# Two of a batch's four scatters move into the next attention step, scatters and gathers stand singly in GpSimd's program, and scale_wqkv goes behind low_part

## The chip, the cores and the metric

The kernel runs on one core of one Trainium2 chip. The metric is the device time in microseconds of one execution. Three executions of the kernel before took 956.85, 956.36 and 955.01 us; the median is 956.36.

The engines are named as the profile names them: PE is TensorE (PEld its weight loads), DVE is VectorE, ACT is ScalarE, POOL is GpSimd, and SP (SyncE) issues most DMAs. SPq and ACTq are the DMA queues of SP and ACT.

## The reference

```python
def reference(x, Wq, bq, Wk, bk, Wv, bv, Wo, bo, qn_w, kn_w, router_w, expert_weights, c, wmod):
    # x: [32, 256, 128]; 16 heads of 8; 32 experts of 128 x 128, two per token
    mod = (silu(c) @ wmod).reshape(32, 6, 1, 128)
    sa, ca, ga, sb, cb, gb = (mod[:, i] for i in range(6))
    ga, gb = at_least(ga, 0.25), at_least(gb, 0.25)        # by size, the sign kept
    h = layernorm(x) * (1 + ca) + sa
    qg = h @ Wq + bq                                       # q, and 16 gates
    Q, K = rmsnorm(q, qn_w), rmsnorm(h @ Wk + bk, kn_w)    # over a head's 8
    attn = softmax(Q @ K.T / sqrt(8))
    out = (attn @ V) * sigmoid(gate)
    x = x + ga * (out @ Wo + bo)
    h = layernorm(x) * (1 + cb) + sb
    rw = softmax(h @ router_w.T)                           # over 32 experts
    out = sum over a token's two best experts of (h * rw_e) @ expert_weights[e]
    return x + gb * out
```

All is float32. The sum over experts is written in the reference as a loop over all 32 with the weights of the others zero.

## The kernel before

Every engine has its own program, written by hand and unrolled in full, and the engines meet only at semaphores. The work goes by batches of 256 tokens (two tiles of 128). The program is a run of steps `s` = 0, 1, ..., each of which handles nine batches at once, each in another phase: `b0` is batch s, `b1` is batch s-1, and so on to `b8`. A step is `attention_step` up to s = 34, and `drain_step` from s = 35 (`DRAIN`) on. In a step, each engine runs a fixed list of small tasks in the order in which they are written there; a task begins with its waits and ends by raising a semaphore. So the order of lines in `attention_step` of POOL is the order of POOL's instructions, and a task that waits holds up all behind it.

The tasks that this text speaks of:

- `scale_wqkv(b0)` on POOL (L766, tile wq_b) scales the weights of the projections by the batch's modulation; PE's `project` (L1914) of the next step uses them.
- `norm_qk(b0, t)` on POOL (L784, qn) ends the step; PE's `transpose_qk` waits for it.
- `low_part(b1)` on POOL (L797, parts) makes the third part of q and k, which are split into three bf16 parts. SP stores the parts in `q_d` and `k_d` in HBM (L602) and loads them again as `q_aug` and `k_aug`, in the layout in which PE's `scores_q` (L1941, mx_ps) of the next batch reads them.
- `scores_q(b, h)` gives the maxima: DVE's `max_head` (L1401, negmax) reads mx_ps. When all 16 heads have theirs, POOL's `max_lead` (L804, mlead), `max_lead_wide` (L811) and `max_rest` (L817, both msplit) split them in two parts, PE's `transpose_max` (L1950) transposes these, ACT copies them (L1087, mrows), and SP stores them into `q_aug` as rows, so that `scores_k` (L1976, st_ps) subtracts the maximum itself. ACT's `exp_head` (L1093, pr) follows.
- `probs_v(b3, g)` on PE (L1990, o_ps) is 16 matmuls for a group of four heads, ACT's `out_transposed` (L1099, oT) copies the result, and the next `probs_v` waits for it, since there is one o_ps.
- `x_plus_bias` (L825, xga), `scale_wo` (L834, wo_b) and `copy_v` (L755, v_aug) are POOL's other small tasks of attention; `scale_ln2` (L841, h2a) and `shift_ln2` (L850, h) write the second norm's result into `h2`.
- The router: DVE finds each token's two best experts (`one_hot`, L1463), POOL makes `mask` (`chosen`, L867), PE counts, and DVE works out the row of each token and expert, `slot` (L1504). `keep_slot` (L899), `keep_index` (L884), `chosen_ranks` (L876, ohr) and `keep_weights` (L891, p_all) keep parts of it; `less_largest` (L858, L859) prepares the softmax.
- `scatter(b, k)` on POOL (L909, xs_d<-h,slot), k = 0 to 3, is one indirect DMA that writes 128 rows of h2 to the places of their experts in HBM: four of them per batch. The first waits for slot. Thirty of the 32 batches go this way, in chunks that end at batches 8, 16, 24 and 30 (`CUTS`); the last two are computed densely.
- When a chunk's rows are all there, SP loads them by units of expert rows (L650, xs_sb<-xs_d), PE transposes and multiplies them (L2121, L2140), and ACT stores the results (ys_d).
- `gather(n, ks)` on POOL (L924, yg<-ys_d,gidx) reads the results back by token, four indirect DMAs per batch, and DVE combines them. In attention steps this is done for one batch per step from s = 25 on; all other batches' gathers are in the drain and behind it. `table` is DVE's reckoning of a chunk's units (L1519 nunit is of it).

In a step with gathers, POOL's list before has gather 0 and scatter 3 of the batch before at its head, and gather 3 and the scatters 0, 1 and 2 near its end, in front of `norm_qk`.

Of the kernel before, what the change touches and what calls it, by code (L numbers as in the profile page):

```python
# [146 lines left out]
def combined_in(s):  # L147

    return COMBINED_IN.get(s, [])
# [71 lines left out]
def build(nc, x, Wq, bq, Wk, bk, Wv, bv, Wo, bo, qn_w, kn_w, router_w, expert_w, c_in, wmod, out):  # L221
# [16 lines left out]
    with ctx:  # L238
# [280 lines left out]
        def past_first(task, b):  # L519

            if b is not None and not (isinstance(b.n, int) and b.n == 0):
                task(b)
# [207 lines left out]
        def _(gp):  # L730
# [97 lines left out]
            @of_batch  # L828
            def scale_wo(b):

                wait(gp, xo_ld[b.par], 32 * (b.nth + 1))
                wait(gp, wo_ps, b.n - 1)
                gp.nop(nofuse=True)
                nc.gpsimd.tensor_tensor(wo_b[:, b.par], wo[:], mod_o[:, b.par, 0, :], ALU.mult).then_inc(wob_d, 1)  # L834
# [93 lines left out]
            def gather_in(s, *ks):  # L928

                for n in combined_in(s):  # L930
                    gather(n, ks)

            def attention_step(s, ahead, b0, b1, b2, b3, b4, b5, b6, b7, b8):

                gather_in(s, 0)
                scatter(b7, 3)
                x_plus_bias(b4)
                scale_wo(b4)
                copy_v(b2)
                keep_slot(b7)  # L940
                past_first(scale_wqkv, b0)
                low_part(b1)
                gather_in(s, 1)
                chosen(b6)
                scale_ln2(b5)
                keep_index(b6)
                gather_in(s, 2)
                chosen_ranks(b6)
                shift_ln2(b5)
                max_lead(b2)  # L950
                max_lead_wide(b2)
                max_rest(b2)
                gather_in(s, 3)
                scatter(b6, 0)
                scatter(b6, 1)
                keep_weights(b8)
                scatter(b6, 2)
                less_largest(b6)
                norm_qk(b0, 0)
                norm_qk(b0, 1)  # L960

            def drain_step(s, ahead, b0, b1, b2, b3, b4, b5, b6, b7, b8):

                if s == DRAIN:
                    scatter(b7, 3)
                gather_in(s, 0, 1)
                for k in range(TOPK * TB):
                    scatter(b6, k)
                gather_in(s, 2, 3)
# [1320 lines left out]
```

## Time and profile before

| | kernel before |
|---|---|
| median of 3 runs | 956.36 us |
| the profiled execution | 961.56 us, of it the span 959.8 us |
| busy share of the span | PE 78%, DVE 71%, ACT 59%, PEld 54%, POOL 53% |
| chain that ended last | PE 40%, DVE 17%, issue 13%, other or unknown queue 11%, DMA 8%, POOL 1% |
| POOL's gathers (L924) | 120, mean 990 ns |
| POOL's scatters (L909) | 120, mean 1004 ns |

The span runs from the first to the last instruction. A busy share is an average over stages: steps with scatters alone, steps with scatters and gathers, and the drain. "Idle before, releaser" is the time for which an engine stood still in front of an operation, and what ended it; "remote" is a releaser that the profile doesn't see as one of the engines, and "issue" is time in which the engine waited for nothing that the profile shows. "issue" in brackets behind a POOL DMA is the gap in front of it.

In the profile a step is read from POOL's `norm_qk` to the next one. Steps 16 to 24 lie from 331 to 529 us; steps 25 to 31, with gathers, from 529 to 702; the last three attention steps from 702 to about 773.

### The profile page before, as it was taken

To read this page: it belongs to the slowest core of one execution; us is meant where nothing else is said; L and a number is where in the kernel's file an instruction comes from. 1 tells how busy PE (TensorE), PEld (TensorE's weight loads), DVE (VectorE), ACT (ScalarE), POOL (GpSimd) and SP (SyncE) were. 2 spreads that over 40 slices of the span, in tenths; PEclk is the share of its full clock that TensorE was granted. 3 is DMA by queue.
4 is the path that set the end of the run, shared out by engine and by line. 5 is a ranking of instruction groups with operands and counts; after the bars stand their busy time and mean duration, and the time that the engine had idled before them with its cause. 6 is when DMAs were issued, how large, how long until landed. Compare 5 with 4: busy or idle time off the path is not lost.

```text
span 959.8 us, 23375 instructions
## 1 busy us (share of the span) xinstructions
PE 746.7 (78%) x6334; PEld 517.7 (54%) x6334; DVE 677.2 (71%) x2015; ACT 562.7 (59%) x1300; POOL 508.2 (53%) x846
## 2 busy tenths in 40 slices
PE   4668989888887899888888888898887753636666
PEld 1235655555554566665656556565665542535665
DVE  4767888778787888788877778799775353602566
ACT  3156877666675788777777777676664622513100
POOL 5112455566555555556455666666664545363353
PEclk8589999999898999999999999999888966857788
DMA  5445455466444667676566767666554343747422
GB/s 155 112 101 152 109 134 154 114 144 150 126 117 115 163 167 190 179 178 173 157 168 173 198 160 185 164 162 165 150 149 122 115 132 101 219 127 220 140 82 83
DMA packets 178001, 141.70 MB, mean 148 GB/s; under 512 B 19540, under 2 KB 162612, under 8 KB 177876
## 3 DMA queue, kind: packets, MB, share of 16 engines
q1 hardware_dynamic: 122804, 99.54, 40.5%
q10 hardware_dynamic: 47392, 24.92, 9.0%
q0 software_dynamic: 7680, 15.74, 6.1%
q8 instruction: 57, 0.93, 0.4%
q14 instruction: 68, 0.56, 0.2%
HBM read 81.77 MB, written 57.80 MB: 145 GB/s over the span
## 4 chain that ended last, share of the span: by engine, by line
PE 40%; DVE 17%; issue 13%; another core or an unknown queue 11%; DMA 8%; SPq 5%; ACT 4%; POOL 1%; DVEq 0%; ACTq 0%; POOLq 0%
PE mx_ps L1941 10%; PE st_ps L1976 8%; PE o_ps L1990 6%; DVE negmax L1401 6%; DMA k_aug<-k_d 4%; PE st_ps L2140 3%; PE misc L1999 3%; DMA k_d<-parts 3%; PE misc L1914 2%; ACT pr L1093 2%; SPq L602 1%; PE mx_ps L2140 1%; SPq L650 1%; PE st_ps L2121 1%
## 5 line engine op out<-in xcount | busy, mean ns | idle before, releaser
L1401 DVE TENSOR_REDUCE negmax<-mx_ps 128x2 f32<-128x512 f32 x512 | 338.5, 686 | 115.6 <-PE mx_ps L1941 58.0
L1093 ACT ACTIVATE pr<-st_ps 128x512 f32<-128x512 f32 x512 | 286.2, 600 | 77.0 <-PE st_ps L1976 72.7
L1941 PE MATMUL mx_ps<-k_aug,q_aug 126*128 126x256 bf16 x1024 | 199.8, 288 | 61.6 <-DVE negmax L1401 28.0
L1976 PE MATMUL st_ps<-q_aug,k_aug 128*128 128x256 bf16 x1024 | 191.1, 286 | 0.6 <-ACT pr L1093 0.3
L1990 PE MATMUL o_ps<-pr,v_aug 128*32 128x256 f32 x2048 | 143.4, 399 | 41.2 <-issue 33.7
L1941 PEld LDWEIGHTS mx_ps<-k_aug,q_aug 126*128 126x128 bf16 x1024 | 84.4, 100 | 151.2 <-issue 140.5
L924 POOL DMA_INDIRECT yg<-ys_d,gidx x120 | 118.8, 990 | 88.9 <-DVE yb L1631 38.8
L909 POOL DMA_INDIRECT xs_d<-h,slot x120 | 120.4, 1004 | 54.6 <-DVE slot L1504 28.7
L1976 PEld LDWEIGHTS st_ps<-q_aug,k_aug 128*128 128x128 bf16 x1024 | 102.3, 105 | 28.9 <-issue 9.7
L1990 PEld LDWEIGHTS o_ps<-pr,v_aug 128*32 128x32 f32 x2048 | 56.5, 111 | 91.9 <-issue 71.9
L1099 ACT ACTIVATE oT<-o_ps 128x256 f32<-128x256 f32 x128 | 49.2, 385 | 85.3 <-remote 49.5
L784 POOL TENSOR_TENSOR qn<-qkvg,rstd 128x256 f32<-128x256 f32 x64 | 39.1, 635 | 80.5 <-DVE rstd L1317 80.5
L797 POOL TENSOR_TENSOR parts<-rest,parts 128x512 bf16<-128x512 f32 x32 | 37.0, 1157 | 58.9 <-ACT parts L1081 58.9
L1914 PE MATMUL misc<-wq_b,hT 128*128 128x400 f32 x128 | 58.7, 547 | 3.2 <-DVE x L1432 2.2
L2121 PE MATMUL st_ps<-ident,xs_sb 128*128 128x128 f32 x248 | 43.0, 304 | 19.7 <-DMA xs_sb<-xs_d 18.1
L1150 ACT ACTIVATE xsT<-st_ps 128x512 f32<-128x512 f32 x62 | 36.6, 595 | 35.8 <-PE st_ps L2121 22.6
L1999 PE MATMUL misc<-ident,oT 128*128 128x128 f32 x256 | 43.8, 300 | 11.3 <-ACT oT L1099 8.4
L2140 PE MATMUL mx_ps<-we,xsT 128*128 x200 | 38.7, 358 | 13.8 <-issue 11.5
L2121 PEld LDWEIGHTS st_ps<-ident,xs_sb 128*128 128x128 f32 x248 | 33.0, 159 | 22.0 <-issue 21.3
L2140 PEld LDWEIGHTS mx_ps<-we,xsT 128*128 128x128 f32 x200 | 35.6, 268 | 16.6 <-issue 16.4
L1370 DVE TENSOR_TENSOR qkvg<-misc,bias_p 128x400 f32<-128x400 f32 x64 | 36.0, 564 | 12.0 <-PE misc L1914 6.5
L1586 DVE TENSOR_TENSOR q_aug<-misc,h2Td 128x512 f32<-128x512 f32 x32 | 21.3, 687 | 32.4 <-remote 23.4
(192 smaller groups left out, 1286.7 us busy)
## 6 DMA issues: line engine op xcount, KB each, us to landing
xs_sb<-xs_d SPq DMA_DIRECT2D x248, 64.0 KB
ys_d<-ys_sb ACTq DMA_DIRECT2D x62, 256.0 KB
q_aug<-q_d SPq DMA_DIRECT2D x64, 192.0 KB
mod_o<-mod_d SPq DMA_DIRECT2D x32, 256.0 KB
bias_p<-bias_d SPq DMA_DIRECT2D x32, 200.0 KB
q_d<-parts SPq DMA_DIRECT2D x32, 192.0 KB
k_d<-parts SPq DMA_DIRECT2D x32, 192.0 KB
k_aug<-k_d SPq DMA_DIRECT2D x64, 96.0 KB
```

What stands on the lines that cost most here:

```text
L909: nc.gpsimd.indirect_dma_start(xs_d[chunk.set], bass.IndirectOffsetOnAxis(ap=slot[:, b.par, k:k + 1], axis=0), h2[:, b.par, k % TB, :], No ...
L924: nc.gpsimd.indirect_dma_start(yg[:, n % FB, k, :], None, ys_d[chunk.c], bass.IndirectOffsetOnAxis(ap=gidx[:, pair:pair + 1], axis=0)).the ...
L1093: nc.scalar.activation(pr[:, h % PR], st_ps[score_bank(b, h)][:], ACT.Exp, scale=SCALE).then_inc(exp_d, 1)
L1099: nc.scalar.activation(oT[:, g, :], o_ps[:, 0:NT], ACT.Copy).then_inc(oT_d, 1)
L1401: v.tensor_reduce(negmax[:, :, h], mx_ps[h % 2][:], AX.X, ALU.max, negate=True).then_inc(mx_d, 1)
L1914: t_.matmul(bank[:, 0:QKVG], hT[:, t * P:(t + 1) * P], wq_b[:, b.par], start=True, stop=True).then_inc(qkv_ps, 1)
L1941: last = t_.matmul(mx_ps[h % 2][:, qc], q_aug[b.par][0:MROW, h, qc * P:(qc + 1) * P], k_aug[b.par][0:MROW, h, :], start=True, stop=True)
L1976: last = t_.matmul(st_ps[score_bank(b, h)][:, kc], k_aug[b.par][:, h, kc * P:(kc + 1) * P], q_aug[b.par][:, h, :], start=True, stop=True)
L1990: last = t_.matmul(o_ps[32 * j:32 * j + VW, 0:NT], v_aug[b.par][:, kc, h, :], pr[:, h % PR, kc, :], start=(kc == 0), stop=(kc == TB - 1))
L1999: last = t_.transpose(bank[:, g * P:(g + 1) * P], oT[:, g, qc * P:(qc + 1) * P], ident[:])
L2121: last = t_.transpose(in_bank(g)[:, k * P:(k + 1) * P], xs_sb[:, g % XB, k, :], ident[:])
L2140: last = t_.matmul(out_bank(g)[:, k * P:(k + 1) * P], xsT[g % XB][:, k * P:(k + 1) * P], we[:, bass.ds(columns[k], P)], start=True, stop=True)
```

## The change

Only POOL's lists are edited. In `attention_step`, scatter 2 of a batch moves from the end of a step to the head of the next one, where scatter 3 already was; scatter 3 moves behind `keep_slot`. Gather 0 goes behind `scale_wo`, and gather 3 in front of `max_lead`. `keep_weights` stands between scatters 0 and 1. `scale_wqkv` goes behind `low_part`. At the first drain step the batch that is in flight has two scatters left instead of one.

```diff
@@ def attention_step(s, ahead, b0, b1, b2, b3, b4, b5, b6, b7, b8):
-                gather_in(s, 0)
-                scatter(b7, 3)
+                scatter(b7, 2)
                 x_plus_bias(b4)
                 scale_wo(b4)
+                gather_in(s, 0)
                 copy_v(b2)
                 keep_slot(b7)
+                scatter(b7, 3)
+                low_part(b1)
                 past_first(scale_wqkv, b0)
-                low_part(b1)
                 gather_in(s, 1)
                 chosen(b6)
                 scale_ln2(b5)
@@
                 gather_in(s, 2)
                 chosen_ranks(b6)
                 shift_ln2(b5)
+                gather_in(s, 3)
                 max_lead(b2)
                 max_lead_wide(b2)
                 max_rest(b2)
-                gather_in(s, 3)
                 scatter(b6, 0)
+                keep_weights(b8)
                 scatter(b6, 1)
-                keep_weights(b8)
-                scatter(b6, 2)
                 less_largest(b6)
                 norm_qk(b0, 0)
                 norm_qk(b0, 1)
@@ def drain_step(s, ahead, b0, b1, b2, b3, b4, b5, b6, b7, b8):
                 if s == DRAIN:
+                    scatter(b7, 2)
                     scatter(b7, 3)
                 gather_in(s, 0, 1)
```

POOL's rows at the head of a step with gathers, before (L766 is scale_wqkv, L797 low_part, L924 a gather, L909 a scatter):

```order
L784 TENSOR_TENSOR qn<-qkvg,rstd 128x2x16x8 x2
L924 DMA yg<-ys_d,gidx 128x128
L909 DMA xs_d<-h,slot 69632x128
L825 TENSOR_TENSOR xga<-x_o,mod_o 128x256
L834 TENSOR_TENSOR wo_b<-wo,mod_o 128x128
L755 COPY v_aug<-qkvg 128x32x8
L899 CAST slot_all<-slot 128x4
L766 TENSOR_TENSOR wq_b<-wqkv,caT 128x400
L797 TENSOR_TENSOR parts<-rest,parts 128x2x256
L924 DMA yg<-ys_d,gidx 128x128
L867 TENSOR_TENSOR mask<-oh 128x64
```

The same place after:

```order
L784 TENSOR_TENSOR qn<-qkvg,rstd 128x2x16x8 x2
L909 DMA xs_d<-h,slot 69632x128
L825 TENSOR_TENSOR xga<-x_o,mod_o 128x256
L834 TENSOR_TENSOR wo_b<-wo,mod_o 128x128
L924 DMA yg<-ys_d,gidx 128x128
L755 COPY v_aug<-qkvg 128x32x8
L899 CAST slot_all<-slot 128x4
L909 DMA xs_d<-h,slot 69632x128
L797 TENSOR_TENSOR parts<-rest,parts 128x2x256
L766 TENSOR_TENSOR wq_b<-wqkv,caT 128x400
L924 DMA yg<-ys_d,gidx 128x128
L867 TENSOR_TENSOR mask<-oh 128x64
```

The pair of gather and scatter behind qn is taken apart, a second scatter stands ahead of low_part, and scale_wqkv has gone behind it.

POOL's rows at the end of the same step, before (L804 to L817 are max_lead, max_lead_wide and max_rest, L891 keep_weights, L858 less_largest):

```order
L850 TENSOR_TENSOR h<-h2a,mod_o 128x256
L804 CAST mlead<-negmax 128x32
L811 CAST msplit<-mlead 128x2x16
L817 TENSOR_TENSOR msplit<-negmax,mlead 128x2x16
L924 DMA yg<-ys_d,gidx 128x128
L909 DMA xs_d<-h,slot 69632x128 x2
L891 TENSOR_TENSOR p_all<-elg,rsum 128x4
L909 DMA xs_d<-h,slot 69632x128
L858 TENSOR_TENSOR dlg<-lg,top 128x2x32
```

and after:

```order
L850 TENSOR_TENSOR h<-h2a,mod_o 128x256
L924 DMA yg<-ys_d,gidx 128x128
L804 CAST mlead<-negmax 128x32
L811 CAST msplit<-mlead 128x2x16
L817 TENSOR_TENSOR msplit<-negmax,mlead 128x2x16
L909 DMA xs_d<-h,slot 69632x128
L891 TENSOR_TENSOR p_all<-elg,rsum 128x4
L909 DMA xs_d<-h,slot 69632x128
L858 TENSOR_TENSOR dlg<-lg,top 128x2x32
```

Behind msplit stand two DMAs with one operation between them, where there were four with one operation between; one of the four now stands ahead of mlead, and one is in the next step.

## Rows read from the trace of the kernel before

**Rows 1.** Busy time, share of the span and instructions of each engine.

```profile
PE 746.7 (78%) x6334; PEld 517.7 (54%) x6334; DVE 677.2 (71%) x2015; ACT 562.7 (59%) x1300; POOL 508.2 (53%) x846
```

**Rows 2.** The chain that ended last, by engine.

```profile
PE 40%; DVE 17%; issue 13%; another core or an unknown queue 11%; DMA 8%; SPq 5%; ACT 4%; POOL 1%; DVEq 0%; ACTq 0%; POOLq 0%
```

**Rows 3.** Two stretches: window, length, each engine's busy time (count), PEclk, DMA share, GB/s.

```profile
331.00:529.00 198.00, 175.90 (x1687) 125.08 (x1684) 162.62 (x484) 153.76 (x359) 111.42 (x207) 0.98 0.67 174
529.00:702.00 173.00, 145.45 (x1320) 100.13 (x1320) 139.17 (x413) 119.59 (x280) 116.00 (x189) 0.94 0.65 170
```

**Rows 4.** Groups by line, 331 to 529 us: busy, mean ns | idle before, releasers.

```profile
L1990 PE MATMUL o_ps<-pr,v_aug 128*32 128x256 f32 x576 | 38.5, 385 | 12.0 <-issue 9.0 <-ACT oT L1099 3.0
...
L1099 ACT ACTIVATE oT<-o_ps 128x256 f32<-128x256 f32 x36 | 13.8, 384 | 14.2 <-remote 9.7 <-PE o_ps L1990 4.5
...
L867 POOL TENSOR_TENSOR mask<-oh 128x64 bf16<-128x64 f32 x9 | 2.9, 319 | 18.0 <-DVE oh L1463 16.3 <-ACT xh L1007 1.7
```

**Rows 5.** Groups by line, 529 to 702 us.

```profile
L1990 PE MATMUL o_ps<-pr,v_aug 128*32 128x256 f32 x448 | 33.4, 420 | 18.5 <-issue 14.1 <-ACT oT L1099 4.4
...
L1099 ACT ACTIVATE oT<-o_ps 128x256 f32<-128x256 f32 x28 | 10.9, 389 | 26.6 <-remote 20.4 <-PE o_ps L1990 6.2
...
L804 POOL CAST mlead<-negmax 128x32 bf16<-128x32 f32 x7 | 1.5, 209 | 7.7 <-DVE negmax L1401 7.7
L867 POOL TENSOR_TENSOR mask<-oh 128x64 bf16<-128x64 f32 x7 | 2.2, 317 | 4.3 <-DVE oh L1463 3.2 <-ACT xh L1007 1.0
```

**Rows 6.** In order of time, step 27: start, duration, engine, operation [idle before].

```profile
590.86 0.21 POOL L804 CAST mlead<-negmax 128x32 bf16<-128x32 f32 x1 [0.59 <-DVE negmax L1401]
...
593.03 1.07 PE L1990 MATMUL o_ps<-pr,v_aug 128*32 128x256 f32 x16
...
594.82 1.23 POOL L909 DMA_INDIRECT xs_d<-h,slot  x1 [0.30 <-issue]
...
597.37 0.38 ACT L1099 ACTIVATE oT<-o_ps 128x256 f32<-128x256 f32 x1 [2.67 <-remote]
```

**Rows 7.** The same, step 29.

```profile
643.49 1.07 PE L1990 MATMUL o_ps<-pr,v_aug 128*32 128x256 f32 x16
...
646.37 0.38 ACT L1099 ACTIVATE oT<-o_ps 128x256 f32<-128x256 f32 x1 [1.16 <-remote]
646.53 1.00 POOL L909 DMA_INDIRECT xs_d<-h,slot  x1 [0.95 <-issue]
```

**Rows 8.** The same, an early step, without scatters.

```profile
108.52 1.07 PE L1990 MATMUL o_ps<-pr,v_aug 128*32 128x256 f32 x16
...
110.15 0.38 ACT L1099 ACTIVATE oT<-o_ps 128x256 f32<-128x256 f32 x1
```

**Rows 9.** The same, step 33, two places.

```profile
745.60 0.40 PE L1950 MATMUL misc<-ident,msplit 128*32 128x128 f32 x2 [0.57 <-POOL msplit L817]
...
754.93 0.38 ACT L1099 ACTIVATE oT<-o_ps 128x256 f32<-128x256 f32 x1 [4.62 <-remote]
```

**Rows 10.** The same, step 30.

```profile
654.38 1.18 DVE L1519 TENSOR_TENSOR nunit<-ucount,unit 128x32 f32<-128x32 int32 x1
...
654.66 0.84 POOL L766 TENSOR_TENSOR wq_b<-wqkv,caT 128x400 f32<-128x400 f32 x1
...
656.50 0.52 PE L1999 MATMUL misc<-ident,oT 128*128 128x128 f32 x3 [1.08 <-DVE rest L1390]
```

**Rows 11.** Four short windows, columns as in rows 3.

```profile
593.00:597.40 4.40, 2.07 (x23) 0.94 (x22) 3.18 (x13) 1.44 (x4) 3.61 (x5) 1.00 0.75 174
597.90:601.30 3.40, 3.40 (x25) 1.96 (x25) 2.83 (x7) 1.13 (x6) 1.40 (x4) 0.50 1.03 248
643.50:646.40 2.90, 1.87 (x23) 0.96 (x22) 2.83 (x13) 1.40 (x4) 1.77 (x2) 1.00 0.39 106
748.70:754.90 6.20, 2.46 (x26) 1.36 (x26) 0.65 (x4) 0.72 (x4) 5.53 (x9) 1.00 0.50 144
```

**Rows 12.** The longest waits by engine: us in total, times, longest.

```profile
PE mx_ps L1941 <- DMA k_aug<-k_d: 22.6, 14, 5.7
```

## The prediction, made before the changed kernel ran

> **What bounds the kernel now.** The page comes first. PE is busy for 78% of the span and POOL for 53% [rows 1]. In the chain that ended last PE holds 40%, "issue" 13%, other sources of unknown queue 11%, and POOL 1% [rows 2]. So POOL, the only engine whose program is edited, bounds nothing by its own length. It matters only through what waits for it, and through when its DMAs go out.
>
> The second view is the table of stretches [rows 3]. From 331 to 529 us nine steps run with four scatters each and no gather (22.0 us a step). From 529 to 702 us seven steps run with four scatters and four gathers each (24.7 us a step). The reader is to see that 2.7 us a step are lost there, that PE's own busy time is no reason (145.45 us in seven steps is 20.8 a step, against 19.5), and that the granted clock is 0.94 there against 0.98.
>
> The third view is the groups by line in the same two stretches. In nine steps without gathers ACT stood idle for 14.2 us before out_transposed (oT, L1099) and PE 12.0 us before probs_v (o_ps, L1990) [rows 4]. In seven steps with gathers it is 26.6 and 18.5 us [rows 5]. Per step that is 1.6 to 3.8 for ACT, and 1.3 to 2.6 for PE. No other group of PE grows so much.
>
> The fourth view is the order of time around one such place [rows 6]. probs_v of group 2 starts on PE at 593.03 and lasts 1.07. oT, which waits for it, starts at 597.37, after 2.67 of idle time "<-remote", and holds up PE's next probs_v. Meanwhile POOL ran DMA_INDIRECT behind DMA_INDIRECT: gather 3 at 592.22, scatters at 593.52, 594.82 and 596.45. The hand-off took 4.34 us. In the seven gather steps I read 5.04, 4.34, 4.34, 5.05, 2.87, 5.80, 3.13. The one of 2.87 (step 29) is the only one in which POOL stood still for 0.95 between two of its DMAs, and oT started in that break [rows 7]. In the first batches, where POOL has no scatter yet, the same hand-off takes 1.63 [rows 8]; in the steps with scatters alone 2.1 to 2.9. So the length of POOL's run of DMAs and the hand-off go together. The profile doesn't prove which causes which.
>
> **The change part by part.** All sums are against the profiled execution, 961.6 us (span 959.8), which is 5.2 above the median of the runs, 956.4. The differences are carried over to the median.
>
> (a) Gather 3 leaves its place ahead of the scatters, and the third scatter goes to the next step. What is left beside the hand-off is one scatter, a small operation (p_all, 0.2), one scatter. If the run of DMAs causes the stall, the seven gather steps fall to the level of those without gathers: PE's idle time 18.5 less 7/9 of 12.0 is 9.2 us. I take 8.0, since two scatters still stand there. The other bound is zero.
>
> (b) Gather 3 now stands in front of max_lead, and max_lead → max_lead_wide → max_rest → transpose_max on PE is a chain for which PE waits. A DMA_INDIRECT of 1.00 and its gap of 0.15 come to 1.15. POOL had 7.7 us idle before mlead in seven steps [rows 5], but unevenly: .60, .57, .59, 1.83, 1.83, 1.44, .80, and step 27 shows 0.59 [rows 6]. In part scale_wqkv (0.84) is added, since low_part no longer stands behind it and the POOL queue up to mask is later by what mask's idle time doesn't cover (.31, .55, .69, .69, .12, 0, .11, worked out from the idle times before mask, 4.3 us in seven steps [rows 5]). That makes msplit late by .86, 1.13, 1.25, .01, 0, 0, .46. PE had slack behind msplit of .56, .51, .56, .01, 0, 0, .23. What is left is .30, .62, .69, 0, 0, 0, .23: +1.9 us. The bounds are +1.9 and, without slack, +3.7. In steps 32 to 34, with no slack (PE waited 0.57 for msplit already [rows 9]), the idle time before mlead is .40 and the delay .75 in two of the steps: +1.5, of which about half falls beside a wait for k_aug. In steps without gathers mask's wait (18.0 us in nine steps [rows 4]) covers the 0.84 whole.
>
> (c) low_part ahead of scale_wqkv. It waits for ACT's middle part and had idle time before it in every step, so that it starts no earlier and no later. wq_b is needed a step later by PE; nobody waits for it. Zero. But in step 30 the DVE operation nunit took 1.18 us where wq_b ran beside it on POOL, and PE then waited 1.08 for DVE's rest [rows 10]. After the change low_part or an idle POOL stands there: −0.8, bounds 0 and −1.0. The Trainium skill, "SBUF — State Buffer", section "SBUF: two separate sides", says that the port pair that DVE and GpSimd share is held by one of them for a whole instruction; by that rule, the trace agrees with 1.18 us for this one. The same section gives PE, ACT and the DMA ports no part in that lock, so by it no DMA of POOL delays PE's hand-off to ACT, and (a) would be worth nothing.
>
> (d) Steps 32 to 34. There gathers and scatters follow one another up to the next step's start, and the last hand-off takes 5.29, 6.21 and 5.45 instead of the usual 1.2; step 33 shows oT at 754.93 after 4.62 idle [rows 9]. After the change qn, xga and wo_b come between. Bounds: 0, and 3 × 4.3 = −13; other waits lie at the same place, so I take −1 each, −3, and with (b)'s half of 1.5 it is −2.2.
>
> (e) Steps without gathers. One scatter less stands beside the hand-off, which takes 2.1 to 2.9 with and 1.6 without scatters. Bounds 0 and −0.35 × 20 = −7. Scatter 2 goes out some 3 us later and scatter 3 some 3 us later in its step, which shift_ln2 (two batches on) and the loads of the experts' rows (a step on) don't see. I take −2. Batches' first scatter and mask wait for DVE as before.
>
> (f) Clock. PE's idle stretches after the long hand-offs are followed by half a clock: at 597.9 PE ran 3.4 us at 0.50 [rows 11]. At 0.98 instead of 0.94, 145.45 us of PE work take 5.9 less; I take a quarter, −1.5, as the waits don't all go. "TensorE: Matmul & The Clock Gate" of the Trainium skill, in Part 1, has the engine throttled by default and released by activity, which is the direction of this row; no number here hangs on it.
>
> (g) Drain. scatter(b7, 2) and (b7, 3) stand at its head together, +1.3 on POOL, where POOL waits for slot anyway: zero.
>
> Sum: −8.0 + 1.9 − 0.8 − 2.2 − 2.0 − 1.5 = −12.6. The saved time is not all kept. A step is also a round trip: low_part, the store of q and k, their load, scores_q of the next step. PE waited 22.6 us in all for k_aug, 14 times [rows 12]; a step that gets shorter finds this wait, as steps 2 to 15 do. I keep 60%: −7.6 us. 961.6 becomes 954.0; the median 956.4 becomes **948.8**.
>
> **The rivals.** First, slower: POOL's DMAs are not what delays the hand-off. For it: the rule of the ports above; and the DMA engines' share was 0.75 in step 27's window and 0.39 in step 29's [rows 11], so that the traffic of the loads may be the cause, and the long and the short hand-off are then told apart by that. Against it: from 748.7 to 754.9, in step 33, the share was only 0.50 and the hand-off 6.21 [rows 11]. Then (a), (d), (e), (f) are nothing and (b) decides, at the chain gather 3 → max_lead → transpose_max: +1.9 + 1.5 − 0.8 = +2.6, 959.0. It decides as soon as gather 3 and the rest of wq_b exceed POOL's idle time before mlead, as they do in four of the seven steps.
>
> Second, no change: the hand-offs get shorter, but PE then meets the k_aug round trip, or the same wait for msplit, and gives back what it saved: −12.6 + 12.6, 956.4. For it: 22.6 us of such waits, PE's 13% "issue" in the chain. Against it: only two of these 14 waits lie after 331 us.
>
> Third, more: all of the sum is kept and the clock comes back whole: −12.6 − 4.4 = −17, 939.4. For it: no k_aug wait in steps 26 to 31.
>
> **How the numbers follow.** Forecast 0.45, slower rival 0.21, no change 0.17, larger gain 0.17. A measurement of this kernel tells 0.2% (1.9 us) from no change. The forecast and the larger gain lie below: 0.62 faster, 0.17 the same, 0.21 slower. The range is from 938 (the larger gain with a little of (d)) to 959.5 (the slower rival, half a us over). The likeliest case's own range is 944 to 953.5: from 40% of the sum kept, with (a) at 4, to all of it.
>
> **What would show it.** In the profile after: ACT's idle time before oT in the gather steps should fall from 3.8 to about 1.6 a step, the hand-off at probs_v(2) from 4.3 to under 3, and the gather steps from 24.7 to about 23.7. PE's wait for msplit should appear in gather steps 25 to 27, a few tenths each. nunit should take 0.2. If oT still waits 3 us and more, (a) is wrong and the first rival holds; if oT's idle time is gone and k_aug waits stand there instead, the second. If the steps without gathers change by more than 0.3 us each, (e) is mis-sized.

## The result, and the profile after

The changed kernel took 901.57 us in the median (901.37 to 902.52), the kernel before in the same session 956.61. The ratio is 0.943, with an interval from 0.939 to 0.947. Forecast were 948.8 and a range from 938 to 959.5: the sign was right, the size seven times too small.

One thing has to be known to read the rest. The kernel before ran in five further sessions, the changed one in two of them. In one of them the kernel before took 945.74 us and the changed one 897.89, ratio 0.948 (0.940 to 0.955), as at first. In the four others the kernel before took 823 to 827 us, and the changed kernel, run in one of these, was slower: 830.13 against 823.29 in the medians, ratio on record 1.012 (1.005 to 1.020). All runs of one session share its state. What the states are the experiments show; I call the first **held** and the second **open**. The two traces of this case's prediction and result are both of the held state.

The profiled execution has a span of 899.9 us, 59.9 less. Its page, the line that answers to [rows 1] and the one that answers to [rows 2]:

```profile
PE 713.3 (79%) x6334; PEld 495.5 (55%) x6334; DVE 679.2 (75%) x2015; ACT 561.3 (62%) x1300; POOL 512.5 (57%) x846
...
PE 33%; DVE 16%; issue 15%; DMA 11%; SPq 10%; POOL 6%; another core or an unknown queue 5%; ACT 3%; POOLq 0%; DVEq 0%; ACTq 0%
```

PE's busy time fell by 33.4 us without one instruction less (x6334 in both), so that is clock: the mean granted clock went from 0.886 to 0.921. The other 26.5 us are time in which PE stood idle.

The stretches of the same steps, as in [rows 3] (window, length, busy times with counts, PEclk, DMA share, GB/s); nine steps without gathers, then seven with:

```profile
315.00:502.00 187.00, 171.86 (x1689) 123.06 (x1688) 163.23 (x485) 153.26 (x359) 112.40 (x207) 1.00 0.73 184
502.00:658.00 156.00, 137.74 (x1326) 96.06 (x1323) 142.33 (x414) 119.48 (x281) 118.76 (x189) 1.00 0.75 189
```

198 us became 187, and 173 became 156, both at a clock of 1.00. The step starts of POOL's norm_qk give all of it: to step 4, 94.5 and 96.3 us (+1.8); steps 5 to 15, 236.3 and 219.0 (−17.3); steps 16 to 24, 198.4 and 187.0 (−11.4); steps 25 to 31, 173.0 and 155.8 (−17.2); the last 257.5 and 241.8 us (−15.7). About half of what was won lies in steps that have no gather. Of the 28.7 us won in steps 5 to 24, some 14 are PE's busy time (187.5 us from 113 to 331 us became 177.5 from 114 to 315, at a clock of 0.92 and 0.97, and 175.9 became 171.9), the rest is idle time that is gone.

The groups that answer to [rows 4], of the changed kernel (L1991 is L1990 of before, and so on, one up), with DVE's max_head above them (busy, mean ns | idle before, releasers):

```profile
L1402 DVE TENSOR_REDUCE negmax<-mx_ps 128x2 f32<-128x512 f32 x144 | 95.7, 687 | 15.3 <-PE mx_ps L1942 14.2
...
L1991 PE MATMUL o_ps<-pr,v_aug 128*32 128x256 f32 x576 | 38.5, 385 | 10.4 <-ACT oT L1100 6.1 <-issue 3.4 <-ACT pr L1094 0.9
...
L1100 ACT ACTIVATE oT<-o_ps 128x256 f32<-128x256 f32 x36 | 13.8, 384 | 12.9 <-remote 8.6 <-PE o_ps L1991 4.2
```

ACT's idle time before oT moved little: 12.9 after 14.2. What moved is DVE's before negmax. Here is its row of the kernel before, from the same answer as [rows 4]; it stood there as the first row, and I didn't read it:

```profile
L1401 DVE TENSOR_REDUCE negmax<-mx_ps 128x2 f32<-128x512 f32 x144 | 95.7, 687 | 26.5 <-remote 16.1 <-PE mx_ps L1941 9.9
```

26.5 became 15.3 us, and "<-remote 16.1" is gone.

The groups that answer to [rows 5]:

```profile
L1991 PE MATMUL o_ps<-pr,v_aug 128*32 128x256 f32 x448 | 30.0, 385 | 3.8 <-issue 3.8
...
L1100 ACT ACTIVATE oT<-o_ps 128x256 f32<-128x256 f32 x29 | 11.1, 383 | 9.2 <-remote 6.3 <-PE o_ps L1991 2.8
...
L1951 PE MATMUL misc<-ident,msplit 128*32 128x128 f32 x14 | 2.7, 278 | 2.5 <-POOL msplit L817 2.5
...
L804 POOL CAST mlead<-negmax 128x32 bf16<-128x32 f32 x7 | 1.5, 219 | 0.3 <-issue 0.3
...
L1520 DVE TENSOR_TENSOR nunit<-ucount,unit 128x32 f32<-128x32 int32 x1 | 0.2, 182 | 0.0
```

PE's wait before probs_v went from 18.5 to 3.8, ACT's before oT from 26.6 to 9.2. POOL now has 0.3 us left before mlead instead of 7.7, PE waits 2.5 for msplit, and nunit takes 0.2. The hand-off at probs_v(2) takes 2.81, 2.88, 2.87, 1.36, 1.30, 2.23 and 2.87 in the seven steps, "under 3" as the prediction said.

The remote waits of the whole span, before and after (us in total, times, longest):

```profile
DVE negmax L1401 <- remote: 49.6, 21, 4.2
ACT oT L1099 <- remote: 49.5, 23, 4.9
...
ACT ys_sb L1155 <- remote: 25.3, 3, 10.0
```

```profile
ACT ys_sb L1156 <- remote: 38.1, 5, 13.5
...
ACT oT L1100 <- remote: 20.3, 16, 2.1
...
DVE negmax L1402 <- remote: 2.6, 2, 1.3
```

DVE's 49.6 us before negmax became 2.6, ACT's 49.5 before oT 20.3. Single gaps can be followed. Batch 20 in the kernel before (start, duration, engine, operation [idle before]):

```profile
500.24 1.07 PE L1990 MATMUL o_ps<-pr,v_aug 128*32 128x256 f32 x16
...
501.51 0.60 PE L1941 MATMUL mx_ps<-k_aug,q_aug 126*128 126x256 bf16 x4
...
502.97 0.99 POOL L909 DMA_INDIRECT xs_d<-h,slot  x1 [0.16 <-issue]
...
503.18 0.38 ACT L1099 ACTIVATE oT<-o_ps 128x256 f32<-128x256 f32 x1 [1.27 <-remote]
...
504.68 1.29 DVE L1401 TENSOR_REDUCE negmax<-mx_ps 128x2 f32<-128x512 f32 x2 [2.54 <-remote]
```

and in the changed kernel:

```profile
476.77 0.59 PEld L1991 LDWEIGHTS o_ps<-pr,v_aug 128*32 128x32 f32 x16 [0.21 <-issue]
...
478.24 0.99 POOL L909 DMA_INDIRECT xs_d<-h,slot  x1 [0.16 <-issue]
...
478.67 0.60 PE L1942 MATMUL mx_ps<-k_aug,q_aug 126*128 126x256 bf16 x4 [0.46 <-DMA k_aug<-k_d]
...
479.67 0.38 ACT L1100 ACTIVATE oT<-o_ps 128x256 f32<-128x256 f32 x1 [1.23 <-remote]
479.75 1.29 DVE L1402 TENSOR_REDUCE negmax<-mx_ps 128x2 f32<-128x512 f32 x2 [1.08 <-PE mx_ps L1942]
```

In the kernel before scores_q's four matmuls start at 501.51 and take 0.60, and DVE sees them at 504.68: 0.72 us behind the end of the third scatter (502.97 + 0.99), though they were done more than 2 us earlier; PE's two updates for them are recorded at 504.65 and 504.70. In the changed kernel there is no third scatter; oT and negmax start 0.44 and 0.52 us behind the end of the second (478.24 + 0.99). So it isn't one hand-off that was late: PE's updates to DVE come late beside POOL's DMAs as well as PE's to ACT. Not every update does: in the kernel before, in the same gap, an update by ACT (pr, at 501.92) and one by DVE (mv, at 502.15) are recorded 0.02 us and less behind their instructions, in the middle of the second scatter.

### The profile page after: what moved, and what is told of

Read it like the earlier page. It is cut to its first block, busy times and chain, and to the rows that moved or that the text cites. A ratio compares the mean times of both kernels' runs of the same rounds, so it can differ in the third digit from the quotient of the medians.

```text
span 899.9 us, 23375 instructions
## 1 busy us (share of the span) xinstructions
PE 713.3 (79%) x6334; PEld 495.5 (55%) x6334; DVE 679.2 (75%) x2015; ACT 561.3 (62%) x1300; POOL 512.5 (57%) x846
## 4 chain that ended last, share of the span: by engine, by line
PE 33%; DVE 16%; issue 15%; DMA 11%; SPq 10%; POOL 6%; another core or an unknown queue 5%; ACT 3%; POOLq 0%; DVEq 0%; ACTq 0%
PE mx_ps L1942 8%; PE o_ps L1991 6%; PE st_ps L1977 6%; DVE negmax L1402 5%; DMA k_aug<-k_d 4%; SPq L650 3%; DMA k_d<-parts 2%; PE misc L1915 2%; DMA mod_o<-mod_d 2%; PE st_ps L2141 2%; SPq L602 2%; PE misc L2000 2%; POOL parts L797 1%; SPq L626 1%
## 5 line engine op out<-in xcount | busy, mean ns | idle before, releaser
L1942 PE MATMUL mx_ps<-k_aug,q_aug 126*128 126x256 bf16 x1024 | 192.2, 279 | 52.0 <-DMA k_aug<-k_d 24.0
L1977 PE MATMUL st_ps<-q_aug,k_aug 128*128 128x256 bf16 x1024 | 180.9, 274 | 1.7 <-issue 1.2
L924 POOL DMA_INDIRECT yg<-ys_d,gidx x120 | 118.2, 985 | 89.0 <-DVE yb L1632 39.9
L1991 PE MATMUL o_ps<-pr,v_aug 128*32 128x256 f32 x2048 | 140.0, 391 | 20.4 <-issue 13.3
L909 POOL DMA_INDIRECT xs_d<-h,slot x120 | 121.7, 1014 | 47.1 <-DVE slot L1505 24.4
L1977 PEld LDWEIGHTS st_ps<-q_aug,k_aug 128*128 128x128 bf16 x1024 | 97.5, 100 | 26.2 <-issue 10.2
L1991 PEld LDWEIGHTS o_ps<-pr,v_aug 128*32 128x32 f32 x2048 | 55.8, 110 | 70.2 <-issue 49.8
L797 POOL TENSOR_TENSOR parts<-rest,parts 128x512 bf16<-128x512 f32 x32 | 37.1, 1160 | 30.6 <-ACT parts L1082 30.2
L1156 ACT ACTIVATE ys_sb<-mx_ps 128x512 f32<-128x512 f32 x25 | 14.9, 597 | 54.8 <-remote 38.1
```

Source lines behind the costliest of these rows:

```text
L797: nc.gpsimd.tensor_tensor(parts[:, :, 2], rest[:], parts[:, :, 1], ALU.subtract).then_inc(lo_d, 1)
L909: nc.gpsimd.indirect_dma_start(xs_d[chunk.set], bass.IndirectOffsetOnAxis(ap=slot[:, b.par, k:k + 1], axis=0), h2[:, b.par, k % TB, :], No ...
L924: nc.gpsimd.indirect_dma_start(yg[:, n % FB, k, :], None, ys_d[chunk.c], bass.IndirectOffsetOnAxis(ap=gidx[:, pair:pair + 1], axis=0)).the ...
L1942: last = t_.matmul(mx_ps[h % 2][:, qc], q_aug[b.par][0:MROW, h, qc * P:(qc + 1) * P], k_aug[b.par][0:MROW, h, :], start=True, stop=True)
L1977: last = t_.matmul(st_ps[score_bank(b, h)][:, kc], k_aug[b.par][:, h, kc * P:(kc + 1) * P], q_aug[b.par][:, h, :], start=True, stop=True)
L1991: last = t_.matmul(o_ps[32 * j:32 * j + VW, 0:NT], v_aug[b.par][:, kc, h, :], pr[:, h % PR, kc, :], start=(kc == 0), stop=(kc == TB - 1))
```

## The experiments

The theories: A, that an indirect DMA which POOL issues holds the other engines' semaphore updates back until shortly behind its end, and DMAs 0.3 us apart merge into one hold; B, that the traffic of the transfers does it. All ratios are to the kernel before in the same session.

**Four in one session.** scatters_only moves two scatters alone:

```diff
-                scatter(b7, 3)
+                scatter(b7, 2)
...
                 keep_slot(b7)
+                scatter(b7, 3)
...
-                scatter(b6, 2)
...
                 if s == DRAIN:
+                    scatter(b7, 2)
                     scatter(b7, 3)
```

> The kernel before, with only scatters 2 and 3 moved (to the head of the next attention step and behind keep_slot); the gathers, scale_wqkv and keep_weights stay. Theory A (an indirect DMA of POOL holds back the semaphore updates of all engines until it ends, and DMAs that follow one another within some 0.3 us merge into one long hold): in the steps without gathers the run of three near probs_v shrinks to two, and DVE's remote wait before negmax (16.1 us in nine steps) goes; that is the 28 us which the whole change brought up to step 24, and in the gather steps a run of three DMAs instead of four is left: 915 to 930 us. Theory B (the traffic of the transfers holds them back, not their issue): the same bytes a little later, at most a third of the gain: 940 or more.

gathers_only moves two gathers alone:

```diff
-                gather_in(s, 0)
                 scatter(b7, 3)
                 x_plus_bias(b4)
                 scale_wo(b4)
+                gather_in(s, 0)
...
+                gather_in(s, 3)
                 max_lead(b2)
                 max_lead_wide(b2)
                 max_rest(b2)
-                gather_in(s, 3)
```

> The kernel before, with only gathers 0 and 3 moved as in the change. Steps up to 24 are as before. Theory A: in steps 25 to 34 the run gather 3, scatters 0 to 2 loses one of four DMAs, and the run at the step's head is split; of the 17 + 12 us that the change brought in these steps, 8 to 15 come: 941 to 948 us. Theory B: 952 to 958, and msplit is later by what the prediction worked out.

spaced_before leaves the order alone and fills the gaps between neighbouring DMAs (the lines that set up the memset's own tile and semaphore are left out here):

```diff
+            def pause(n=320):
+
+                if len(paused) > 1:
+                    gp.wait_ge(idle_d, len(paused) - 1)
+                nc.gpsimd.memset(idle_t[:, len(paused) % 2, 0:n], 0.0).then_inc(idle_d, 1)
+                paused.append(0)
...
                 gather_in(s, 0)
+                if s > 24:
+                    pause()
                 scatter(b7, 3)
...
                 gather_in(s, 3)
+                if s > 24:
+                    pause()
                 scatter(b6, 0)
+                if s > 5:
+                    pause()
                 scatter(b6, 1)
                 keep_weights(b8)
+                if s > 5:
+                    pause()
                 scatter(b6, 2)
```

> The kernel before with its order untouched, and a small memset of 128x320 on POOL between DMAs of an attention step that stood directly behind one another (or with only keep_weights between). Same bytes, same order, more work on POOL. Theory A: the updates get through between two DMAs, and 15 to 45 us go, 910 to 940. Theory B, or that the number of DMAs near the hand-off decides and not their distance: 956 or slower, by the memsets' time.

space_drain puts the same memset behind each gather and scatter of the drain and behind it, in the changed kernel:

```diff
-                gather_in(s, 0, 1)
+                for n in combined_in(s):
+                    for k in (0, 1):
+                        gather(n, (k,))
+                        pause()
                 for k in range(TOPK * TB):
                     scatter(b6, k)
-                gather_in(s, 2, 3)
+                    if b6 is not None and b6.n < NS:
+                        pause()
+                for n in combined_in(s):
+                    for k in (2, 3):
+                        gather(n, (k,))
+                        pause()
...
-                gather(n, range(TOPK * TB))
+                for k in range(TOPK * TB):
+                    gather(n, (k,))
+                    pause()
```

> The changed kernel with the same memset behind each gather and scatter of the drain steps and behind them, where now up to 16 gathers follow one another and ACT and DVE show remote waits of 8.9, 13.5, 16.1 and 12.8 us. Theory A: these waits end after one DMA instead of sixteen; 10 to 35 us less than the changed kernel, 867 to 892. Theory B: no gain, 900 to 912.

The session was open, and all four expectations, made for a kernel that takes 956 us, missed: before 827.22 us. scatters_only 841.82 (1.018, 1.013 to 1.023), gathers_only 830.80 (1.006, 1.003 to 1.009), spaced_before 833.31 (1.011, 1.006 to 1.015), space_drain 847.36 (1.025, 1.021 to 1.029). Theory B says nothing about why the same bytes should take 956 us in one session and 827 in another; theory A as I had put it was wrong too, since POOL's DMAs held nothing back here. What differs is seen in the traces. I counted the semaphore updates of all engines that a trace records (those of DMAs left out), from 150 to 640 us, per us of time behind the start of a DMA_INDIRECT, for DMAs that stand alone by 1.2 us on either side and for those that the next one follows within 0.45 us:

```
                     alone, 0.3-1.2 us   1.5-2.2 us   followed, 0.3-1.2 us   1.5-2.2 us
before        held         1.7              8.8              0.9                1.5
after         held         2.1              8.2              0.9                2.0
after_again   held         2.3              8.2              0.8                1.7
gathers_only  open         5.3              8.9              5.0                6.7
low_first     open         5.8              8.9              5.2                6.8
after_3       open         5.5              8.5              4.9                5.6
```

In the held state the updates beside a DMA thin out to a third, and come at the full rate behind it; where a second DMA follows they stay thin. In the open state they don't. The table mixes two things, updates that are late and updates that are missing from the trace: the first trace of the kernel before has 4,815 semaphore updates other than those of DMAs and that of the changed kernel 4,739, where low_first and after_3 in the open state, with as many instructions, have 5,465 and 5,467. That updates are late, and not only unrecorded, is seen one by one: of 140 updates by PE that were due beside a POOL DMA (from 0.3 us behind its start to 0.1 behind its end, in the same stretch; the next update of the same semaphore is taken for it), the trace of the kernel before has 20 within 0.1 us, 97 later and 23 not within 4 us; in low_first 216 of 218 are there within 0.1 us. The engines' starts say the same, and in the 14 open traces no wait at all is put down to "remote". The same batch 20 in the open state, in low_first (below), whose three scatters stand as in the kernel before:

```profile
461.25 1.07 PE L1990 MATMUL o_ps<-pr,v_aug 128*32 128x256 f32 x16
...
462.63 0.96 POOL L909 DMA_INDIRECT xs_d<-h,slot  x1 [0.30 <-issue]
...
462.77 0.60 PE L1941 MATMUL mx_ps<-k_aug,q_aug 126*128 126x256 bf16 x4
462.82 0.37 ACT L1099 ACTIVATE oT<-o_ps 128x256 f32<-128x256 f32 x1
463.19 1.29 DVE L1401 TENSOR_REDUCE negmax<-mx_ps 128x2 f32<-128x512 f32 x2
```

probs_v starts at 461.25 and oT at 462.82, in the middle of a scatter: 1.57 us instead of 2.94.

**Four in a held session.** The next session had the kernel before at 945.74 us.

> The changed kernel, unaltered, beside the kernel before. In the first four experiments the kernel before took 827 us, not 956, and in their traces every semaphore update came 0.01 us behind its instruction, whatever POOL did. Theory A2: whether POOL's DMAs hold back the updates is a state of the chip or machine, and the change pays only there: where the kernel before takes about 956 the change gives 0.94, where it takes about 827 it gives 1.00 to 1.02 (scatters_only gave 1.018). Rival C: the change pays everywhere and only scatters_only doesn't: 0.97 or less on either chip.

> The kernel before, unaltered, for its trace beside the others. Ratio 1.00. Theory A2: with about 827 us, oT starts 1.2 us behind probs_v's start and DVE has no remote wait before negmax; with about 956 both are as in the first trace.

> As spaced_before: the kernel before with a memset between neighbouring DMAs of POOL in attention steps. Where the kernel before takes 956, theory A says 910 to 940, theory B (traffic) 956 or more. Where it takes 827, about 833 again.

> As space_drain: the changed kernel with a memset behind each gather and scatter of the drain. Where the kernel before takes 956, theory A says 10 to 35 us less than the changed kernel, theory B no less. Where it takes 827, about 847 again, which is slower than the changed kernel by the memsets' time.

after_again 897.89, ratio 0.948 (0.940 to 0.955). before_again 946.99, 1.001 (0.997 to 1.005). spaced_before_2 889.46, **0.940 (0.933 to 0.947)**. space_drain_2 858.41, **0.906 (0.901 to 0.912)**. So the kernel before, in its own order, with 78 memsets more on POOL, gains as much as the whole change: 56 us, more than the 15 to 45 that theory A gave. No transfer is moved ahead or left out in it. That tells A from B, and it shows the cause in the held state. In its trace, batch 20:

```profile
493.60 1.07 PE L2005 MATMUL o_ps<-pr,v_aug 128*32 128x256 f32 x16
493.65 1.03 POOL L909 DMA_INDIRECT xs_d<-h,slot  x1 [1.25 <-DVE slot L1519]
...
494.68 0.38 POOL L937 MEMSET idle_t<- 128x320 f32 x1
...
495.17 0.38 ACT L1114 ACTIVATE oT<-o_ps 128x256 f32<-128x256 f32 x1
495.23 0.97 POOL L909 DMA_INDIRECT xs_d<-h,slot  x1 [0.17 <-issue]
```

The first scatter ends at 494.68; oT starts at 495.17, 0.49 us behind it and just ahead of the next scatter at 495.23. The distance between two DMAs grew from 0.30 to 0.55 us, which is enough to let the updates through. Steps 16 to 24 take 20.4 us each (22.0 in the first trace of the kernel before, 20.8 in that of the changed one), those with gathers 21.8 (24.7 and 22.3): the gain lies in the same steps as the change's.

In the drain the holds are longer. The changed kernel's ACT and POOL:

```profile
786.18 0.60 ACT L1151 ACTIVATE xsT<-st_ps 128x512 f32<-128x512 f32 x1 [2.62 <-issue]
...
797.19 0.95 POOL L924 DMA_INDIRECT yg<-ys_d,gidx  x1 [0.30 <-issue]
800.32 0.60 ACT L1156 ACTIVATE ys_sb<-mx_ps 128x512 f32<-128x512 f32 x1 [13.54 <-remote]
```

POOL issues sixteen gathers from 778.24 to 798.14, 0.30 apart. ACT waits 13.54 us, until 2.2 us behind the last. Some updates do get through in the run (ACT started operations at 781.34, 782.96 and 786.18), so that the hold isn't a closed door. With a memset behind each gather the remote waits of the whole span are

```profile
ACT oT L1117 <- remote: 14.2, 14, 1.5
...
ACT ys_sb L1173 <- remote: 9.3, 6, 2.4
```

9.3 us in total before ys_sb instead of 38.1, the longest 2.4 instead of 13.5. 39.5 us came from 84 gaps of 0.25 us more; theory A had said 10 to 35.

**Four in an open session.**

> The kernel before in its own order, with the memset between neighbouring DMAs of POOL both in the attention steps and in the drain. Theory A, where POOL's DMAs hold the updates back (the kernel before near 950): spaced_before gave 0.940 and the drain's memsets took another 0.041 from the changed kernel, so 0.895 to 0.905. Where they don't (near 827): 1.03 to 1.04. Theory B (traffic): no less than 0.94.

> As scatters_only: only scatters 2 and 3 moved. Where the updates are held, theory A says steps up to 24 as short as in the changed kernel (20.1 and 20.9 us), and the gather steps between the two: 0.96 to 0.97. Where they are not held: 1.018 again.

> As gathers_only: only gathers 0 and 3 moved. Where the updates are held, theory A says steps up to 24 as in the kernel before (21.8 and 22.3 us) and 8 to 15 us less behind them: 0.984 to 0.992. Where they are not held: 1.006 again.

drain_short_pause is space_drain with `def pause(n=8)`:

> The changed kernel with a memset of 128x8 instead of 128x320 behind each DMA of the drain: as many instructions between the DMAs, but the distance from one's end to the next one's start stays near 0.3 us instead of 0.55. Theory A (the updates come through about 0.35 us behind a DMA's end, so a distance decides): 0.94 to 0.95, as the changed kernel without memsets. Theory A3 (any instruction between two DMAs lets the updates through): 0.90 to 0.91, as space_drain_2.

Before 826.95. space_all (spaced_before's and space_drain's memsets in the kernel before) 843.16, 1.022 (1.015 to 1.029); scatters_only_2 1.016 (1.009 to 1.023); gathers_only_2 1.006 (1.002 to 1.010); drain_short_pause 1.012 (1.005 to 1.019). Where nothing is held a memset only costs; space_all cost 2.2%, where 3 to 4% were expected. drain_short_pause never met a held session, and so its question has no run of its own. But the held traces have a like case: keep_weights (p_all, 0.21 us) stands between two scatters, 0.40 us apart. From 0.25 to 0.6 us behind the first one's end the updates come there at 1.9 per us in the kernel before (21 places) and 2.4 in the changed kernel (19), with the memset at 0.55 us at 7.2 (spaced_before_2, 35), and with nothing between at 0.30 us at 0.4 (30); in the open state, in low_first, p_all's places have 5.7. So not any instruction opens the gap, which speaks for the distance; a memset and p_all differ in more than length, so it isn't proven.

**Four more, open again.**

> The changed kernel beside the kernel before once more. Where updates are held (before near 950): 0.945 again. Where they are not (near 827): as scatters_only's 1.016 and gathers_only's 1.006 add up, 1.015 to 1.03.

> As scatters_only_2. Where updates are held: 0.96 to 0.97, steps up to 24 as short as in the changed kernel. Where not: 1.016.

wqkv_back is the changed kernel with

```diff
-                low_part(b1)
                 past_first(scale_wqkv, b0)
+                low_part(b1)
```

> The changed kernel with scale_wqkv ahead of low_part again. The prediction put its move at nothing but nunit's 0.8 us. Theory A, held: within 3 us of the changed kernel, since it stands between scatter 3 and low_part and moves no DMA. A rival: where low_part waits for nothing any more, 0.84 us a step come back on the round trip of q and k, so up to 0.84 x 25 = 21 us slower than the changed kernel in either state.

> As space_all. Where updates are held: 0.895 to 0.905. Where not: 1.022 again.

Before 823.29. after_3 830.13, 1.012 (1.005 to 1.020). scatters_only_3 840.83, 1.023 (1.017 to 1.030). wqkv_back 840.50, 1.023 (1.016 to 1.030). space_all_2 841.81, 1.021 (1.015 to 1.027). wqkv_back's rival came true: with scatter 3 in front of low_part, scale_wqkv ahead of it costs 10 us. PE's waits for k_aug (total, times, longest) in after_3 and in wqkv_back:

```profile
PE mx_ps L1942 <- DMA k_aug<-k_d: 30.4, 29, 6.1
```

```profile
PE mx_ps L1942 <- DMA k_aug<-k_d: 39.2, 29, 6.2
```

8.8 us of the 10 (up to 21 had been allowed). In the open state low_part is on the path of the round trip: scatters_only_3, which lacks the swap too, has 43.2 us of this wait and loses as much.

**The last two, open.**

```diff
-                past_first(scale_wqkv, b0)
                 low_part(b1)
+                past_first(scale_wqkv, b0)
```

> The kernel before with one edit: low_part ahead of scale_wqkv, no DMA moved. Where updates come through (before near 825): undoing it in the changed kernel cost 10 us, of which as much should come here as low_part waits less: the kernel before has scatter 3 ahead of them at the step's head, not one more right in front of low_part, so 0 to 10 us less, 0.988 to 1.0. The prediction's own theory (low_part waits for ACT anyhow, nothing gained): 1.00. Where updates are held: 0.99 to 1.0.

> As scatters_only_3. Where updates are held: 0.96 to 0.97, with steps up to 24 as short as in the changed kernel. Where not: 1.02.

low_first, the kernel before with the swap alone, 825.36 against 824.83: 1.000 (0.997 to 1.004). scatters_only_4 843.70, 1.022 (1.017 to 1.028). So the swap gains nothing by itself; it pays for the scatter that the change puts in front of low_part. What is left of the change in the open state, +7 us, is by gathers_only the gathers: ratio 1.006, 3 to 4 us, and 17.3 us of weight loads waiting for msplit where low_first has 12.4. The rest, some 3 us, was not taken apart.

No version beats both kernels in both states. In the held state space_drain_2 is the fastest measured (0.906), in the open state the kernel before, with low_first level. space_all, which theory A puts at 0.895 to 0.905 in the held state, never met one; nor did scatters_only, gathers_only, wqkv_back and low_first.

## Why the prediction was wrong

**The mechanism was named, one of its hand-offs was read and the others not.** "The length of POOL's run of DMAs and the hand-off go together" was right, and spaced_before_2 shows which causes which in the held state. But the prediction took the hand-off PE to ACT at probs_v(2) for all of it. DVE's wait before negmax is the same thing, 49.6 us of "remote" in the span, and was not in the sum. By the steps the 59.9 us divide into +1.8 (to step 4), −28.7 (steps 5 to 24, term (e)), −17.2 (steps 25 to 31, (a) to (c)), −16.9 (up to the last oT of attention, (d)) and +1.1 (behind it, (g)), the clock of (f) in each.

**(a), gather steps: mis-sized by reading one line.** Taken 8.0, bound 9.2 us. PE's idle time before o_ps fell by 14.7; the stretch by 17.2. The bound was no bound, since the level of the steps without gathers was itself held.

**(e), steps without gathers: the step that failed.** Taken −2, bounds 0 and −7; measured −28.7 us over steps 5 to 24, the largest part of the result. The prediction priced it by what oT's hand-off could win (2.1 to 2.9 against 1.6). oT won 1.3 us in steps 16 to 24 (14.2 to 12.9), and its hand-off at probs_v(2) still takes 2.2 to 2.9 there; negmax won 11.2. The rows of one view were read for the line in question and not from the top. The prediction's own sign for this, more than 0.3 us a step, came: 1.3 in steps 16 to 24 and 1.6 in steps 5 to 15. Also, "2.1 to 2.9" is read from steps 16 to 24; in steps 6 to 15 the same hand-off took 1.8 to 4.2.

**(d), steps 32 to 34: the whole bound came and more.** Taken −3 of −13. From the end of step 31 to the last oT of attention 73.3 us became 56.5: −16.9. The three last hand-offs themselves, 5.29, 6.21 and 5.45, became 1.13, 1.20 and 1.22: −13.4, just the bound. The reason for taking a quarter of it ("other waits lie at the same place") rested on no row.

**(f), clock: a quarter taken, much more than the whole came.** Taken −1.5. PE's busy time fell by 7.7 us in steps 25 to 31 and by 33.4 in the span, since stretches at half the clock had stood in every attention stage with holds, also from 113 to 331 us, where the mean was 0.92 and is now 0.97 (114 to 315). The sum had the clock in one stretch only.

**The share kept.** 60% was to remain, because PE would meet the k_aug wait. It went from 22.6 us to 24.0: next to nothing was given back in the held state. "Only two of these 14 waits lie after 331 us" was misread: it is four (at 390, 548, 571 and 722 us, 4.5 us in all), one of them in step 26; that there are few and short ones holds. In the open state the wait is 30.4 us in after_3 and 31.1 in low_first; whether a saving would be given back there, no run shows.

**(b), msplit: right.** +1.9 foreseen from idle time and slack; PE waited 2.5 us for msplit and 1.4 for mask in the gather steps. In the open state it is most of what the gathers cost: 4.0 us in gathers_only against 1.1 in low_first, of 3.6.

**(c), the swap and nunit: wrong in the place of the wait.** nunit fell from 1.18 to 0.18 us, but the 0.8 us were not won. A few operations later in the same step DVE's ubeg, like nunit a difference of two tiles, now takes 2.32 us, where it took 0.72 in the kernel before and 0.19 at its shortest. It ends 0.06 us behind low_part and scale_wqkv, as nunit ended 0.06 behind scale_wqkv, and PE then waits 1.96 us for DVE instead of 1.08:

```profile
618.68 2.32 DVE L1524 TENSOR_TENSOR ubeg<-uend,nunit 128x32 f32<-128x32 f32 x1
618.97 1.17 POOL L797 TENSOR_TENSOR parts<-rest,parts 128x512 bf16<-128x512 f32 x1
620.09 0.85 POOL L766 TENSOR_TENSOR wq_b<-wqkv,caT 128x400 f32<-128x400 f32 x1
...
621.83 0.38 PE L1942 MATMUL mx_ps<-k_aug,q_aug 126*128 126x256 bf16 x2 [1.96 <-DVE negmax L1402]
```

"It starts no earlier and no later" holds for the swap alone (low_first 1.000), but not beside the other edit: the change puts scatter 3 in front of low_part, and wqkv_back shows that the swap then saves 10 us in the open state. Adding prices of single edits missed that; in the held state it was not tried.

**(g), drain: right.** Priced at zero for its two scatters; behind the last oT of attention 184.2 us became 185.3. The holds of the drain itself, larger than all of (a) (39.5 us came from spacing them), are untouched by the change and were overlooked.

**The rivals.** The slower one said that POOL's DMAs are not what delays the hand-off, and that then (b) decides. In the held state it is refuted. In the open state it is nearly what happens: no wait is "remote", and the kernel is slower, by 6.8 us in the medians (ratio 1.012), where +2.6 us (0.3%) were worked out. The Trainium skill, "SBUF — State Buffer", section "SBUF: two separate sides", names, among the engines' ports, only the pair of DVE and GpSimd as shared; by it PE's hand-off to ACT and DVE doesn't depend on POOL. In the open state the traces agree (oT starts in the middle of a scatter, 1.57 us behind probs_v); in the held state they don't (4.34 us, and 0.940 by memsets alone), and the measurement decides. It isn't shown that a port is what the updates wait for. The third rival, "more", had the right direction and a third of the size.

**What stays open.** What puts a session into the one state or the other; it isn't the kernel, as both states hit the same kernels, and it isn't the chip, as far as its number tells: the first open session, the held one behind it and the last open one were all on chip 9, the other two open ones on 3 and 12 (the record has no number for the session of the prediction). By which way POOL's DMA holds the updates back. Whether the recording of the trace has a part in it: every timed execution has a span and a granted clock from the profiler, and the traces of the held state are the ones that lack records, so no run shows that the hold is there without it. How the 55 us divide between scatters and gathers by a run in the held state: the stages say that up to step 24 all of it is the scatters with the swap and keep_weights' new place, since there is no gather; from step 25 on it was not taken apart.

## What to carry to other kernels

Read a view of waits from the top, and sum one releaser ("remote") over all lines before pricing one of them: if an engine's updates come late, all who wait for them are late. Keep GpSimd's indirect DMAs apart by some half a microsecond of other work or of nothing where other engines hand work to one another at that time and the trace shows "remote" waits; where it shows none the same memsets cost 1 to 2%. So measure it in more than one session, since the same memsets gave 0.94 in one and 1.01 in another. Price edits that touch one queue together: a task that waits for nothing new alone may be late behind the other edit.

## What the runs showed of the hardware that was not expected

The same kernel took 956 and 946 us in two sessions and 823 to 827 in four, and within a session it stayed. In the held state updates of semaphores beside a DMA_INDIRECT of POOL are recorded at a third of the rate (1.7 to 2.3 per us against 5.3 to 5.8), in part because they are late, until some 0.3 to 0.7 us behind its end, and in part because they are missing from the trace. With DMAs 0.30 us apart this goes on for the whole run of them, up to 13.5 us for one wait, though some updates get through. A memset of 0.38 us between them, which makes the distance 0.55, lets them through; p_all at a distance of 0.40 mostly doesn't. In the open state nearly every update is recorded 0.01 to 0.04 us behind its instruction, DMA or not.
